# Eight edge columns per comparison in the edge stage of a window-attention and graph-expert kernel

## Chip, cores and metric

One Trainium2 chip, one core. The metric is the device time in microseconds of one execution; of several runs the median is taken.

## What is computed

The input is a (32, 32, 32, 128) tensor: 32 images of 1024 tokens with 128 features. The reference runs two window attentions (the second on shifted windows) and adds them to `x`. Then it runs a graph-attention gate over 32768 nodes and 524288 edges plus 32768 self loops, and four experts mixed by the top two gate scores. The part that matters here is the gate, which reduces over the edges by their destination, and the experts:

```python
src = jnp.concatenate([edge_index[0], loops]); dst = jnp.concatenate([edge_index[1], loops])
e = jax.nn.leaky_relu(a_src[src] + a_dst[dst], negative_slope=0.2)
ee = jnp.exp(e - segment_max(e, dst)[dst]); denom = segment_sum(ee, dst)
agg = segment_sum(h[src] * (ee / denom[dst]), dst) + b_gat
...
hh = jax.nn.gelu(x @ W1[ei] + b1[ei], approximate=False)
out = out + g[..., None] * (hh @ W2[ei] + b2[ei])
```

## The kernel before

Three stages run one after the other: `attention` (windows, node rows, and a sort of the edges by destination), `edges`, and `combine` (gates, mixing, output). The change is in `edges`.

`edges` has 64 passes (`CHUNKS`). The first two and the last two are written out straight, the 60 between them are a hardware loop (`Fori`) of two passes per turn. Each engine has its own order within pass c:

- VectorE (DVE, lines 1336 to 1431 and the pass at the end of that block): `decode(c+1)` turns sorted keys into row numbers `src`; `counts(c)`; `outputs(c)`; `math(c)` with the scans over 68 sorted edges per partition.
- `counts` builds a histogram of the unsorted destinations. A destination is split into its low 7 bits and its high 8 bits. For each of the `HC` = 64 edge columns of a pass, L1418 compares the row 0..127 with the low part, one number per partition, and so writes a one-hot column `ohl` (128x128); L1419 does it for the high part, `ohh` (128x256). Both lie in a ring of `RING` = 8 columns. TensorE multiplies `ohl` by `ohh` (L1651) and accumulates in `cbank`; at the pass's end L1421 adds `cbank` to `hist`.
- TensorE (PE): the 64 one-hot matmuls, then 8 matmuls `hbank` of the experts' first layer (L1658), then 32 matmuls `ybank` of the second (L1667). In fp32 each of these is two loads and two matmuls in the trace. ScalarE (ACT) applies gelu to each `hbank` (L1627, two banks in turn); VectorE adds the bias to each of four `ybank` results (L1431, `yo`).
- GpSimd (POOL): after `decode(c+1)` it issues 68 indirect DMAs (L1602), the gathers of node rows `G` for pass c+1, double-buffered. `math(c)` waits for the gathers of its own pass and for `outputs(c)`, which stands ahead of it on VectorE.
- SyncE (SP) loads keys, destinations and tokens and stores results.

The semaphore `s_oh` tells TensorE of each finished column, `s_ohp` tells VectorE of each multiplied one; a column may be overwritten when the one eight columns back has been multiplied.

Of the kernel before, what the change touches and what calls it, by code (L numbers as in the profile page):

```python
# [21 lines left out]
ALU = mybir.AluOpType  # L22
# [3 lines left out]
P = 128  # L26
# [1133 lines left out]
HC = EDGES // P // CHUNKS  # L1160
# [5 lines left out]
LOW = -1.0e38  # L1166
HI = NODES // P
MCH, LCH, ACH = 0, GHEADS, 2 * GHEADS
RING = 8
CONSTANTS = 9  # L1170
EH = GDIM // GHEADS
VCH = NROW - LCH
# [2 lines left out]
def edges(nc, sorted_keys, node_rows, edge_index, tnT, W1, b1, W2, b2, state_rows, expert_out, endi):  # L1175
# [3 lines left out]
    with ExitStack() as ctx:  # L1179
        def sb(name, shape, dt=F32):  # L1180
            return ctx.enter_context(nc.sbuf_tensor("edge_" + name, shape, dt))
# [4 lines left out]
        def sem(name):  # L1186
            return ctx.enter_context(nc.semaphore("edge_" + name))
# [26 lines left out]
        dlf = sb("dlf", [P, 2, HC])  # L1214
        io = sb("io", [P, HI], I32)
        iob = sb("iob", [P, HI], BF16)
        ohl = sb("ohl", [P, RING, P], BF16)
        ohh = sb("ohh", [P, RING, HI], BF16)
        hist = sb("hist", [P, HI])
# [48 lines left out]
        s_oh = sem("s_oh")  # L1268
        s_ohp = sem("s_ohp")
# [31 lines left out]
        def first_of(b, i, n=1):  # L1301
            return isinstance(i, int) and 2 * i + b < n
# [7 lines left out]
        def _(dve):  # L1310
# [8 lines left out]
            def link(ins, at):  # L1319

                ins.then_inc(s_step, 1)
                st.k += 1
                dve.wait_ge(s_step, at + st.k)
# [83 lines left out]
            def counts(b, i, at):  # L1407
                c = 2 * i + b
                dve.wait_ge(s_dx[b], 16 * i + 16)
                dve.tensor_scalar(dlo[:, 0, :], dx[b][:, :], P - 1, None, ALU.bitwise_and)  # L1410
                link(dve.tensor_scalar(dlo[:, 1, :], dx[b][:, :], 7, None, ALU.logical_shift_right), at)
                link(dve.tensor_copy(dlf[:, :, :], dlo[:, :, :]), at)
                dve.sem_inc(s_dxr, 1)
                for t in range(HC):
                    if t >= RING or not first_of(b, i):

                        dve.wait_ge(s_ohp, c * HC + t - RING + 1)
                    dve.tensor_scalar(ohl[:, t % RING, :], iob[:, 0:P], dlf[:, 0, t:t + 1], None, ALU.is_equal)  # L1418
                    dve.tensor_scalar(ohh[:, t % RING, :], iob[:, :], dlf[:, 1, t:t + 1], None, ALU.is_equal).then_inc(s_oh, 1)  # L1419
                dve.wait_ge(s_ohp, (c + 1) * HC)  # L1420
                dve.tensor_tensor(hist[:, :], cbank[b][:, 0:HI], hist[:, :], ALU.add).then_inc(s_hs, 1)  # L1421

# [216 lines left out]
        @block.tensor  # L1639
        def _(pe):  # L1640
            pe.wait_ge(s_w, 64)

            def body(b, i):
                c = 2 * i + b

                if not first_of(b, i, 2):
                    pe.wait_ge(s_hs, c - 1)
                for t in range(HC):

                    pe.wait_ge(s_oh, c * HC + t + 1)  # L1650
                    pe.matmul(cbank[b][:, 0:HI], ohl[:, t % RING, :], ohh[:, t % RING, :],  # L1651
                              start=(t == 0), stop=(t == HC - 1)).then_inc(s_ohp, 1)

                pe.wait_ge(s_xt[b], 16 * i + 16)
                for k in range(EXPERTS * HB):
                    if k >= 2 or not first_of(b, i):
                        pe.wait_ge(s_ge, c * EXPERTS * HB + k - 1)
                    pe.matmul(hbank[k % 2][:, :], w1[:, k // HB, (k % HB) * P:(k % HB + 1) * P], xt[b][:, :],  # L1658
                              start=True, stop=True).then_inc(s_l1, 1)

                pe.wait_ge(s_ge, (c + 1) * EXPERTS * HB)
                for t in range(UTILES):
                    if t >= 2 or not first_of(b, i):
                        pe.wait_ge(s_y, c * UTILES + t - 1)
                    for x in range(EXPERTS):
                        for h in range(HB):
                            last = pe.matmul(ybank[t % 2][:, x * P:(x + 1) * P], hid[:, x * HB + h, t * P:(t + 1) * P],  # L1667
                                             w2[:, x, h, :], start=(h == 0), stop=(h == HB - 1))
                    last.then_inc(s_l2, 1)

            chunks(pe, body)

            pe.wait_ge(s_hs, CHUNKS)
            pe.wait_ge(s_c, CONSTANTS)
            pe.matmul(hbank[0][:, 0:HI], tri[:, :], hist[:, :], start=True, stop=True)
            pe.matmul(hbank[1][:, 0:HI], ones[:, :], hist[:, :], start=True, stop=True).then_inc(s_pe, 1)
            pe.wait_ge(s_end, mark["x3"])
            for k in range(3):
                last = pe.transpose(cbank[0][0:VCH, k * P:(k + 1) * P], x3[:, k, :], ident[:, :])
            last.then_inc(s_pe, 1)  # L1680
            pe.wait_ge(s_end, mark["V"])
            pe.transpose(cbank[1][:, 0:VCH], most[:, 0:P], ident[0:VCH, 0:VCH])
            pe.transpose(cbank[1][:, VCH:2 * VCH], total[:, 0:P], ident[0:VCH, 0:VCH]).then_inc(s_pe, 1)
# [248 lines left out]
```

## Time and profile before

| | us |
|---|---|
| median of 3 runs | 11302.15 |
| lowest, highest | 11301.26, 11305.25 |
| the profiled execution | 11406.52 |
| its span | 11404.8 |

Engines' busy shares of the span: PE 37%, DVE 47%, ACT 19%, POOL 43%. In the 40 slices of the page, the first seven are the attention stage, the last three or so hold `combine`; the nearly even stretch between is the edge stage. There PE, DVE and POOL are each busy two to four tenths of the time and the granted TensorE clock is half in most slices. So no engine is full there, and a reader must look at one pass in order of time: what each engine does, and what its idle time before each instruction was ended by.

### The profile page before, as it was taken

Reading aid. Unit: us, or ns where it says so; the run is one execution under the profiler, and the core shown is the slowest. Engines: PE = TensorE matmul, PEld = TensorE weight load, DVE = VectorE, ACT = ScalarE, POOL = GpSimd, SP = SyncE. Lnnn points to the kernel's source line nnn. Section 1 sums busy time; section 2 is a strip of 40 time slices with the busy share of each in tenths; the row PEclk is TensorE's granted clock in tenths of the full one; section 3 lists DMA queues with packets and bytes.
Section 4 is the critical chain, followed back from the end, with each engine's and each line's share of the span. In section 5 each row is a group of like instructions: output and inputs, shape, how many; then the busy total and the mean of one; then the engine's idle time right before and its main releaser. Section 6 shows DMA issues by size and latency. Waiting matters only on the chain. (4 is left out here: it accounts for less than half of the span.)

```text
span 11404.8 us, 104675 instructions
## 1 busy us (share of the span) xinstructions
PE 4230.9 (37%) x31385; PEld 2300.7 (20%) x31448; DVE 5397.3 (47%) x14623; ACT 2169.7 (19%) x4631; POOL 4862.3 (43%) x5600
## 2 busy tenths in 40 slices
PE   6899987223222222222222223322222222222300
PEld 4666665011111111111111111111111111111100
DVE  9999998233333333333333333333333333333437
ACT  5777775000000000000000000000000000000015
POOL 3222221644444444444444444444444444444261
PEclk8999998555555555555555555555555555555555
DMA  1222222000001110100000000000110100010147
GB/s 51 59 59 59 59 59 64 16 22 22 22 22 25 27 22 22 22 22 22 22 22 22 22 22 22 22 22 22 29 23 22 22 22 22 22 22 22 32 136 220
DMA packets 503856, 419.15 MB, mean 37 GB/s; under 512 B 160546, under 2 KB 400338, under 8 KB 502866
## 3 DMA queue, kind: packets, MB, share of 16 engines
q1 hardware_dynamic: 355842, 356.89, 9.9%
q0 software_dynamic: 147552, 56.96, 4.3%
q8 instruction: 186, 3.05, 0.1%
q14 instruction: 276, 2.26, 0.1%
HBM read 203.44 MB, written 176.45 MB: 33 GB/s over the span
## 5 line engine op out<-in xcount | busy, mean ns | idle before, releaser
L1602 POOL DMA_INDIRECT edge_G<-node_rows,edge_src x4352 | 4113.1, 945 | 4601.1 <-DVEq L1359 3293.7
L1651 PE MATMUL edge_cbank<-edge_ohh,edge_ohl 128*128 128x256 bf16 x4096 | 1481.1, 396 | 6159.5 <-DVE edge_ohh L1419 5207.8
L1419 DVE TENSOR_SCALAR edge_ohh<-edge_iob,edge_dlf 128x256 bf16<-128x256 bf16 x4096 | 1220.1, 300 | 2169.1 <-issue 2168.9
L1418 DVE TENSOR_SCALAR edge_ohl<-edge_iob,edge_dlf 128x128 bf16<-128x128 bf16 x4096 | 1107.5, 271 | 2159.5 <-issue 2114.5
L1651 PEld LDWEIGHTS edge_cbank<-edge_ohh,edge_ohl 128*128 128x128 bf16 x4096 | 434.4, 106 | 7199.7 <-DVE edge_ohh L1419 5948.5
L1627 ACT ACTIVATE edge_hid<-edge_hbank,edge_b1c 128x512 f32<-128x512 f32 x512 | 351.7, 687 | 7228.5 <-PE edge_hbank L1658 7199.7
L1431 DVE TENSOR_TENSOR edge_yo<-edge_ybank,edge_b2r 128x512 f32<-128x512 f32 x256 | 177.0, 692 | 1003.5 <-PE edge_ybank L1667 940.1
L569 POOL TENSOR_TENSOR attn_nw<-attn_st 128x8 f32<-128x8 f32 x64 | 42.4, 662 | 1409.6 <-DVE attn_st L1024 1409.6
L1658 PE MATMUL edge_hbank<-edge_xt,edge_w 128*128 128x512 f32 x1024 | 601.4, 738 | 29.2 <-ACT edge_hid L1627 16.3
L1667 PE MATMUL edge_ybank<-edge_w,edge_hid 128*128 128x128 f32 x4096 | 477.7, 278 | 76.3 <-ACT edge_hid L1627 62.0
L1667 PEld LDWEIGHTS edge_ybank<-edge_w,edge_hid 128*128 128x128 f32 x4096 | 465.7, 193 | 130.0 <-issue 100.6
L1035 DVE TENSOR_TENSOR attn_keys<-attn_keys 128x1024 f32<-128x1024 f32 (+1 forms) x340 | 477.2, 1404 | 8.7 <-DVE attn_keys L1040 0.5
L1040 DVE TENSOR_TENSOR attn_keys<-attn_keys 128x1024 f32<-128x1024 f32 (+1 forms) x340 | 475.9, 1400 | 0.1
L1125 DVE TENSOR_REDUCE attn_mx<-attn_score 128x16 f32<-128x1024 f32 (+1 forms) x272 | 314.5, 1156 | 86.3 <-PE attn_score L892 52.8
L892 PE MATMUL attn_score<-attn_km,attn_qT 64*64 64x256 f32 x4096 | 293.5, 400 | 86.5 <-DVE attn_S L1127 77.4
L1127 DVE TENSOR_TENSOR attn_S<-attn_score,attn_mx 128x1024 f32<-128x1024 f32 (+1 forms) x272 | 316.0, 1162 | 9.3
L1793 POOL DMA_INDIRECT comb_srow<-state_rows,end_index x256 | 248.1, 969 | 130.8 <-issue 77.4
L926 PE MATMUL attn_out<-attn_vx,attn_pT 128*64 128x34 f32 x8192 | 297.5, 228 | 14.0 <-DVE attn_att L1114 14.0
L911 PE MATMUL attn_turn<-attn_ident,attn_S 128*128 128x128 f32 x2048 | 292.4, 286 | 0.8 <-ACT attn_pT L758 0.8
L758 ACT ACTIVATE attn_pT<-attn_turn 128x1024 f32<-128x1024 f32 (+1 forms) x272 | 268.0, 985 | 130.1 <-PE attn_turn L911 128.0
L751 ACT ACTIVATE attn_S<-attn_S 128x1024 f32<-128x1024 f32 (+1 forms) x272 | 276.9, 1018 | 29.1 <-DVE attn_S L1127 27.4
L1658 PEld LDWEIGHTS edge_hbank<-edge_xt,edge_w 128*128 128x128 f32 x1024 | 205.6, 232 | 378.0 <-ACT edge_hid L1627 272.3
(268 smaller groups left out, 6001.4 us busy)
## 6 DMA issues: line engine op xcount, KB each, us to landing
edge_G<-node_rows,edge_src POOLq DMA_INDIRECT x4352
expert_out<-edge_yo SPq DMA_DIRECT2D x64, 1024.0 KB
comb_ye<-expert_out SPq DMA_DIRECT2D x32, 2048.0 KB
state_rows<-edge_O SPq DMA_DIRECT2D x64, 816.0 KB, 3.6
attn_km<-attn_kT SPq DMA_DIRECT2D x1024, 32.0 KB, 2.0
attn_xin<-in_x SPq DMA_DIRECT2D x32, 512.0 KB, 4.4
attn_xres<-in_x SPq DMA_DIRECT2D x32, 512.0 KB, 5.4
x_rows<-attn_x SPq DMA_DIRECT2D x32, 512.0 KB, 3.4
```

The lines of the kernel that those rows point to most:

```text
L926: last = pe.matmul(out_bank[e * WTOK:(e + 1) * WTOK, j % OUT_SLOTS, c:c + VW], pT[j % 2][:, st, g, e * WTOK:(e + 1) * WTOK], vx[st][:, 2 * ...
L1035: return dve.tensor_tensor(out, a, b, ALU.min)
L1040: return dve.tensor_tensor(out, a, b, ALU.max)
L1125: dve.tensor_reduce(top, scores, AX_X, ALU.max).then_inc(s_mx, 1)
L1127: dve.tensor_tensor(S[j % RING_S][:, :, lo:hi, :, :].rearrange("p a s h k -> p a (s h) k"), scores, top.unsqueeze(3).to_broadcast([P, 2, ( ...
L1418: dve.tensor_scalar(ohl[:, t % RING, :], iob[:, 0:P], dlf[:, 0, t:t + 1], None, ALU.is_equal)
L1419: dve.tensor_scalar(ohh[:, t % RING, :], iob[:, :], dlf[:, 1, t:t + 1], None, ALU.is_equal).then_inc(s_oh, 1)
L1602: pool.indirect_dma_start(G[b][:, t, :], None, node_rows, bass.IndirectOffsetOnAxis(ap=src[b][:, t:t + 1], axis=0)).then_inc(s_g[b][2 * t ...
L1627: act.activation(hid[:, k, :], hbank[k % 2][:, :], ACT.Gelu, bias=b1c[:, k:k + 1]).then_inc(s_ge, 1)
L1651: pe.matmul(cbank[b][:, 0:HI], ohl[:, t % RING, :], ohh[:, t % RING, :], start=(t == 0), stop=(t == HC - 1)).then_inc(s_ohp, 1)
L1658: pe.matmul(hbank[k % 2][:, :], w1[:, k // HB, (k % HB) * P:(k % HB + 1) * P], xt[b][:, :], start=True, stop=True).then_inc(s_l1, 1)
L1667: last = pe.matmul(ybank[t % 2][:, x * P:(x + 1) * P], hid[:, x * HB + h, t * P:(t + 1) * P], w2[:, x, h, :], start=(h == 0), stop=(h == H ...
```

## The change

VectorE no longer compares one column at a time with a number per partition. One `tensor_tensor` compares two broadcast tensors and writes eight columns of `ohl` (128x1024), a second one writes eight of `ohh` (128x2048). The ring grows from 8 to 16 columns. `s_oh` now counts groups of eight, and TensorE waits once per group; it still reports each matmul on `s_ohp`, and VectorE waits before a group until the group two back has been multiplied.

```diff
-RING = 8
+WIDE = 8
+RING = 2 * WIDE
...
-                for t in range(HC):
+                for t in range(0, HC, WIDE):
                     if t >= RING or not first_of(b, i):
 
-                        dve.wait_ge(s_ohp, c * HC + t - RING + 1)
-                    dve.tensor_scalar(ohl[:, t % RING, :], iob[:, 0:P], dlf[:, 0, t:t + 1], None, ALU.is_equal)
-                    dve.tensor_scalar(ohh[:, t % RING, :], iob[:, :], dlf[:, 1, t:t + 1], None, ALU.is_equal).then_inc(s_oh, 1)
+                        dve.wait_ge(s_ohp, c * HC + t + WIDE - RING)
+                    r = t % RING
+                    dve.tensor_tensor(ohl[:, r:r + WIDE, :], iob[:, 0:P].unsqueeze(1).to_broadcast([P, WIDE, P]),
+                                      dlf[:, 0, t:t + WIDE].unsqueeze(2).to_broadcast([P, WIDE, P]), ALU.is_equal)
+                    dve.tensor_tensor(ohh[:, r:r + WIDE, :], iob[:, :].unsqueeze(1).to_broadcast([P, WIDE, HI]),
+                                      dlf[:, 1, t:t + WIDE].unsqueeze(2).to_broadcast([P, WIDE, HI]), ALU.is_equal).then_inc(s_oh, 1)
                 dve.wait_ge(s_ohp, (c + 1) * HC)
...
                 for t in range(HC):
 
-                    pe.wait_ge(s_oh, c * HC + t + 1)
+                    if t % WIDE == 0:
+                        pe.wait_ge(s_oh, c * (HC // WIDE) + t // WIDE + 1)
                     pe.matmul(cbank[b][:, 0:HI], ohl[:, t % RING, :], ohh[:, t % RING, :],
                               start=(t == 0), stop=(t == HC - 1)).then_inc(s_ohp, 1)
```

How the order of the instructions changes on two engines. First VectorE inside the loop, in `counts`, before the change; a REGISTER_ALU works out the number that the wait of L1417 compares with:

```order
L1418 TENSOR_SCALAR edge_ohl<-edge_iob,edge_dlf 128x128
L1419 TENSOR_SCALAR edge_ohh<-edge_iob,edge_dlf 128x256
L1417 REGISTER_ALU
L1418 TENSOR_SCALAR edge_ohl<-edge_iob,edge_dlf 128x128
L1419 TENSOR_SCALAR edge_ohh<-edge_iob,edge_dlf 128x256
```

In the changed kernel VectorE has in `counts`, here in a pass written out straight, from the preparation of the destinations on (of the eight pairs of comparisons the first two are shown):

```order
L1411 TENSOR_SCALAR edge_dlo<-edge_dx 128x64
L1412 TENSOR_SCALAR edge_dlo<-edge_dx 128x64
L1413 CAST edge_dlf<-edge_dlo 128x128
L1420 TENSOR_TENSOR edge_ohl<-edge_iob,edge_dlf 128x1024
L1422 TENSOR_TENSOR edge_ohh<-edge_iob,edge_dlf 128x2048
L1420 TENSOR_TENSOR edge_ohl<-edge_iob,edge_dlf 128x1024
L1422 TENSOR_TENSOR edge_ohh<-edge_iob,edge_dlf 128x2048
```

So 128 comparisons of a pass become 16. TensorE in the loop had, before:

```order
L1650 ISA
L1651 MATMUL edge_cbank<-edge_ohh,edge_ohl 128x256
L1650 REGISTER_ALU
L1651 MATMUL edge_cbank<-edge_ohh,edge_ohl 128x256
L1650 REGISTER_ALU
```

and has now:

```order
L1655 ISA
L1656 MATMUL edge_cbank<-edge_ohh,edge_ohl 128x256 x8
L1655 REGISTER_ALU
L1656 MATMUL edge_cbank<-edge_ohh,edge_ohl 128x256 x8
L1655 REGISTER_ALU
```

The 64 matmuls of a pass stay, each still with its own weight load; seven in eight of the waits, and of the register instructions ahead of them, are gone. No other engine's instructions change.

## Rows read from the trace of the kernel before

**Rows 1.** The page: the span, and busy time of each engine.
```profile
span 11404.8 us, 104675 instructions
PE 4230.9 (37%) x31385; PEld 2300.7 (20%) x31448; DVE 5397.3 (47%) x14623; ACT 2169.7 (19%) x4631; POOL 4862.3 (43%) x5600
```

**Rows 2.** Timeline of POOL: start, duration, idle before and releaser; four gathers.
```profile
2332.27 0.94 POOL L1602 DMA_INDIRECT edge_G<-node_rows,edge_src  x1 [48.14 <-DVEq L1359]
...
5087.93 0.94 POOL L1602 DMA_INDIRECT edge_G<-node_rows,edge_src  x1 [53.35 <-DVEq L1359]
...
5171.69 0.95 POOL L1602 DMA_INDIRECT edge_G<-node_rows,edge_src  x1 [0.30 <-issue]
...
10612.19 0.94 POOL L1602 DMA_INDIRECT edge_G<-node_rows,edge_src  x1 [52.66 <-DVEq L1359]
```

**Rows 3.** Timeline of DVE, the pass that begins at 5087.93.
```profile
5088.26 0.28 DVE L1419 TENSOR_SCALAR edge_ohh<-edge_iob,edge_dlf 128x256 bf16<-128x256 bf16 x1
...
5114.80 0.38 DVE L1418 TENSOR_SCALAR edge_ohl<-edge_iob,edge_dlf 128x128 bf16<-128x128 bf16 x1 [1.11 <-issue]
5116.20 0.29 DVE L1419 TENSOR_SCALAR edge_ohh<-edge_iob,edge_dlf 128x256 bf16<-128x256 bf16 x1 [1.02 <-issue]
...
5183.63 0.28 DVE L1419 TENSOR_SCALAR edge_ohh<-edge_iob,edge_dlf 128x256 bf16<-128x256 bf16 x1
...
5187.22 0.28 DVE L1419 TENSOR_SCALAR edge_ohh<-edge_iob,edge_dlf 128x256 bf16<-128x256 bf16 x1
...
5205.90 0.69 DVE L1431 TENSOR_TENSOR edge_yo<-edge_ybank,edge_b2r 128x512 f32<-128x512 f32 x1 [1.09 <-PE edge_ybank L1667]
```

**Rows 4.** Timeline of ACT: first gelu of that pass; last of the pass begun at 7990.30.
```profile
5189.86 0.69 ACT L1627 ACTIVATE edge_hid<-edge_hbank,edge_b1c 128x512 f32<-128x512 f32 x1 [114.87 <-PE edge_hbank L1658]
5197.65 0.69 ACT L1627 ACTIVATE edge_hid<-edge_hbank,edge_b1c 128x512 f32<-128x512 f32 x1 [0.17 <-PE edge_hbank L1658]
...
8097.55 0.69 ACT L1627 ACTIVATE edge_hid<-edge_hbank,edge_b1c 128x512 f32<-128x512 f32 x1 [0.17 <-PE edge_hbank L1658]
```

**Rows 5.** Timelines of DVE, PE and ACT in the first pass, while 136 gathers run.
```profile
2091.07 0.42 DVE L1419 TENSOR_SCALAR edge_ohh<-edge_iob,edge_dlf 128x256 bf16<-128x256 bf16 x1 [1.16 <-issue]
2109.99 0.42 DVE L1421 TENSOR_TENSOR edge_hist<-edge_cbank,edge_hist 128x256 f32<-128x256 f32 x1 [18.50 <-remote]
...
2098.11 0.40 PE L1651 MATMUL edge_cbank<-edge_ohh,edge_ohl 128*128 128x256 bf16 x1 [2.40 <-remote]
2100.91 0.40 PE L1651 MATMUL edge_cbank<-edge_ohh,edge_ohl 128*128 128x256 bf16 x1 [2.40 <-remote]
...
2132.43 2.07 PE L1658 MATMUL edge_hbank<-edge_xt,edge_w 128*128 128x512 f32 x2 [3.53 <-ACT edge_hid L1627]
...
2131.70 0.69 ACT L1627 ACTIVATE edge_hid<-edge_hbank,edge_b1c 128x512 f32<-128x512 f32 x1 [4.92 <-remote]
2137.29 0.69 ACT L1627 ACTIVATE edge_hid<-edge_hbank,edge_b1c 128x512 f32<-128x512 f32 x1 [4.90 <-remote]
```

**Rows 6.** Windows, first gather to first gap: length, PE, PEld, DVE, ACT, POOL, clock, DMA.
```profile
2199.42:2210.15 10.73, 8.62 (x25) 2.60 (x25) 10.37 (x57) 0.00 (x0) 8.29 (x9) 0.50 0.47 135
5087.93:5096.50 8.57, 5.63 (x16) 1.66 (x16) 7.52 (x40) 0.00 (x0) 6.66 (x7) 0.50 0.20 47
10612.19:10624.26 12.07, 8.82 (x26) 2.62 (x26) 11.07 (x60) 0.00 (x0) 9.33 (x10) 0.50 0.39 115
10824.60:10926.34 101.74, 0.00 (x0) 0.00 (x0) 18.98 (x30) 0.00 (x0) 77.36 (x81) 0.50 0.55 165
```

**Rows 7.** Windows at the end of the pass begun at 5087.93, same columns.
```profile
5187.00:5191.00 4.00, 4.00 (x7) 1.67 (x7) 0.92 (x4) 0.69 (x1) 0.00 (x0) 0.50 0.00 0
5191.00:5193.00 2.00, 2.00 (x4) 0.80 (x3) 0.00 (x0) 0.70 (x2) 0.00 (x0) 0.62 0.00 0
5193.00:5206.60 13.60, 12.02 (x74) 8.41 (x72) 2.77 (x6) 5.39 (x7) 0.00 (x0) 1.00 0.00 0
```

**Rows 8.** Groups by form: `combine` during gathers (10905 to 10926); edge stage (5000 to 6000).
```profile
L1821 DVE TENSOR_TENSOR comb_agg<-comb_srow,comb_l 128x1024 f32<-128x1024 f32 x1 | 1.2, 1226 | 0.0
...
L1397 DVE TENSOR_TENSOR edge_msg<-edge_G,edge_wbank 128x1088 f32<-128x1088 f32 x7 | 19.6, 2794 | 0.0
```

## The prediction
> **What bounds the kernel now.** I read the page first. No engine is full over the span [rows 1], so the order in time decides. POOL's timeline gives the passes: the sixty passes of the loop lie between the first gathers at 2332.27 and 10612.19 [rows 2], so one takes 8279.92 / 60 = 138.0 us. In one pass POOL issues its 68 gathers from 5087.93 to 5171.69 [rows 2], 1.25 us apart, and then waits more than 50 us for VectorE's next decode.
>
> From here on times are offsets from a pass's first gather. VectorE's timeline [rows 3] falls into three. Until about +8.6 the comparisons come as one pair per 0.36 us. Then each one takes 1.40 us from start to start (5114.80, 5116.20) though it is busy for 0.3 to 0.4, and the idle time before it is ended by nothing that the trace names ("issue"). At 5183.63, which is +95.7, the pace is back: ten more pairs to 5187.22 are 0.36 us apart. I call +8.6 to +95.5 the slow stretch. It ends 11 us after the last gather was issued, and 95.5 / 68 is 1.40 us per gather. I read that as something that each gather occupies for 1.40 us, and that lets one instruction of each engine through in that time. After the slow stretch: the remaining columns, eight gelus from +101.9 to +110.4 [rows 4], the last `yo` done at +118.7 [rows 3], the scans, the next decode. Only this tail can shrink, as long as the slow stretch itself keeps its length.
>
> **Who sets the pace in the slow stretch.** This decides the case, and rows 5 show it in the first pass. VectorE starts its last comparison at 2091.07 and is done. TensorE's matmuls still come 2.80 us apart (2098.11, 2100.91), and VectorE learns of the last one only at 2109.99, 9 us later. After that each gelu comes 5.6 us after the one before (2131.70, 2137.29); one gelu needs two loads and two matmuls. So TensorE reports one instruction per 1.40 us, loads and matmuls alike: 2.80 us per one-hot column, 5.6 per gelu. VectorE, with two comparisons per column, has the same 2.80. **The change takes away VectorE's share and leaves TensorE's 64 loads and 64 matmuls.** In the slow stretch a column still costs 2.80 us.
>
> **What precedes the slow stretch.** Rows 6 give the instructions started between the first gather and the first gap. In passes written out straight: 25 + 25 + 57 + 9 = 116 in 10.7 us and 26 + 26 + 60 + 10 = 122 in 12.1 us. In a loop pass 16 + 16 + 40 + 7 = 79 in 8.6 us, to which one register instruction per wait comes, some 38, so 117. In `combine` the first gap stands 101.7 us after the first gather, with 81 + 30 = 111. The count agrees, the time doesn't, so I take the fast beginning to last for about 118 instructions.
>
> **The change part by part.** (1) Comparisons. Each now makes 1024 or 2048 elements. A comparison of two tensors isn't in the edge stage's rows at this size; the nearest are a broadcast multiplication of 1024 elements at 1.23 us, and one of 1088 over strided data at 2.79 us [rows 8]. Operands and results here are dense or broadcast, so I take 1.2 and 2.3, 3.5 us per group of eight, 28 us per pass; the strided row gives 7.9 and 63 us. At the low end the rate of the present comparisons (0.36 us per column) gives 2.9 and 23 us. All three are below 95.5 us, so in the loop the choice costs nothing; the cover is the gathers. Only the last pass has no gathers: there 64 × 0.36 = 23 becomes 28, which **adds 5 us** (up to 40).
>
> (2) Instructions before the slow stretch. A group now has 2 comparisons, 16 loads and matmuls and 2 register instructions, 20 instead of 48. With some 12 others (what SyncE issues, VectorE's rows ahead of the comparisons) and POOL's 0.8 per us, 118 are reached after 4.6 groups, 37 columns, at about +18 instead of 16 columns at +8.6. The other 27 cost 27 × 2.80 = 76 us and are reported by +94.
>
> (3) The end of the slow stretch. Today some ten columns are left at +95.5 and the first gelu comes at +101.9. Now TensorE has multiplied all 64, and the first two `hbank` as well, when it ends: the first gelu starts at +95.7. That is 6.2 us earlier, but not all is kept. The granted clock is 0.50 during the gathers and rises only near +104.6, after some 9 us of unbroken matmuls [rows 7], and a `hbank` takes 2.07 us at the low clock [rows 5]. Four more take until +104.7 and two until +106.6, so the last gelu ends at +107.3 instead of +110.4: **3.1 us saved per pass.** In the pass at 7990.30, whose last gelu ends at +107.9 [rows 4], the same sum with its earlier rise of the clock gives 3.2.
>
> (4) The rest. The ring of 16: VectorE needs the group two back; the report of column 48, the last it waits for, comes at +49, long before it matters. `ybank`, `yo`, the scans and the decode stay as they are. The first pass keeps its time, since its outputs wait for 136 gathers either way. The straight passes at 2199.42 and 10612.19 have only one column left at +95.5 today, and lose about 1.3 us each to the low clock.
>
> **Sum:** 60 × 3.1 = 186, less 2.6 and 5, is 178 us. From the profiled execution's 11406.5 that makes 11228.5; its like runs had a median of 11302.15, 0.9% lower, so the slow stretch must be in them too, and I forecast 11302 − 178 = **11124, say 11125.**
>
> **The rivals.** *A. The gathers hold a port that the new form doesn't need.* The present comparisons are of the one-source kind; rows 3 show them stretched beside gathers, which this would explain. The Trainium skill (SBUF — State Buffer, Who interferes with whom) says that `tensor_scalar` in a 2-port mode and a GpSimd instruction block each other, and that `tensor_tensor` has no such mode, though with two SBUF inputs it still contends with a GpSimd instruction that reads SBUF. By that rule the port is what costs 1.40 us, and VectorE would be free of it. As a mechanism: counts 28 us, gelus and `yo` 17, scans 16, decode 6, together 67, below POOL's 68 × 1.25 = 85 or 95. A pass would take 85 to 95 us and the kernel 8120 to 8720. Against it: during the first 8.6 us the same comparisons run at 0.36 a pair beside gathers [rows 3, 6], and TensorE, which has no part in such a lock, shows 2.80 alone [rows 5]. The same rule's clause on two inputs would let the new comparisons wait for gathers; rows 8 show 1.23 us beside gathers, hence no cost.
>
> *B. Only instructions that report count.* Then a column costs TensorE 1.40 us or less, the one-hots end early, and the gelus run inside the slow stretch at 5.6 us. At +95.5 only `ybank` and `yo` are left, about 10 us with the low clock: last `yo` at +105.6 instead of +118.7, 60 × 13 = 780, so 10520. Rows 5 speak against it: a gelu with one report takes as long as two columns with two. A milder form, more than 45 columns before the slow stretch, saves one or two gelus' time more, to about 10900.
>
> *C. Slower.* The slow stretch begins by time, not by count. Place: column 48. VectorE writes its last group only when column 48 is reported. With 16 columns back at +8.6 that is 8.6 + 32 × 2.80 = +98.2, so the end at +95.5 releases it. Then 3.5 us for the group, which nothing covers, 2.3 for its matmuls and 2.07 for the first `hbank` bring the first gelu to +103.5, and the last ends near +113.1: 2.7 us more per pass, 11475. It decides from 19 columns down (92 us is where the wait must be over). For it: the slow stretch begins between +8.6 and +12.1 in every pass of the edge stage; against it, `combine`'s 101.7 us.
>
> *D. No change.* Savings below 0.4 us a pass: the early gelus lose all they gain to the low clock, for instance if TensorE's pauses between them keep it low for some microseconds longer. That the change does less than it says I leave out: the order shows 16 comparisons for 128.
>
> **How the numbers follow.** Forecast (10,980 to 11,250) 0.50; B and its mild form 0.13; A 0.07; C 0.19; D 0.11. The range reaches from 10850, the mild form of B, to 11450, nearly all of C; beyond lie A, B proper and C's last part, under 0.2 together. Faster by over 0.2% (23 us, about what a measurement of this kernel can tell) has 0.70, within it 0.11, slower 0.19.
>
> **What would show it.** In the changed profile: L1420 near 1.2 and L1422 near 2.3 us, 512 of each; first gathers 134.9 us apart instead of 138.0; a first gelu at +95.7 and a last one ending near +107; PE's one-hot matmuls done well before +95 and the rise of the clock near +104. If first gathers are 95 us apart or less, A holds; with a last `yo` near +105, B; with a group of comparisons after +95.5, C. I am wrong at the root if VectorE's own 112 vanished comparisons shorten the slow stretch itself.

## The result and the profile after

| | before | after |
|---|---|---|
| median, us | 11301.7 (4 runs, 11286.9 to 11305.3) | 10907.96 (4 runs, 10903.5 to 10911.2) |
| profiled execution, us | 11406.5 | 10905.7 |
| mean pass of the loop, us | 138.0 | 129.9 |
| instruction packets (queue q14) | 276 | 95 |

The ratio is 0.9652, interval 0.9637 to 0.9667: 394 us faster where 178 were forecast. The kernel before is slower on the chips that the experiments ran on (11398 to 11409), the changed one hardly (10935.9), and there the ratio is 0.9595 (0.9579 to 0.9611). The two profiled executions differ by 500.8 us, and the account below is of these two; the profiled one of the kernel before is as long as the runs on the experiments' chips and 105 us longer than the runs of the table. The mean pass is worked out from the first gathers of the loop's first pass and of the pass behind the loop: before, 8279.9 / 60; after, (10122.0 − 2325.5) / 60.

The page of the changed kernel, the lines that answer to [rows 1], the instruction queue and two groups (busy time, mean ns, then idle time before):

```profile
span 10903.9 us, 90850 instructions
PE 3927.3 (36%) x31448; PEld 2592.5 (24%) x31448; DVE 5142.4 (47%) x7455; ACT 2174.8 (20%) x4631; POOL 5887.7 (54%) x5600
...
q14 instruction: 95, 0.78, 0.0%
...
L1606 POOL DMA_INDIRECT edge_G<-node_rows,edge_src x4352 | 5132.4, 1179 | 3102.1 <-DVEq L1360 1794.1
```

POOL is busier by 1025 us with the same 5600 instructions; of the others only the loads of TensorE (PEld) grew by much, by 292 us. A gather's mean went from 945 to 1179 ns, although nothing of POOL's was changed. Its timeline in the pass that begins at 4665.46 (start, duration, then idle before and its releaser) says where:

```profile
4665.46 0.95 POOL L1606 DMA_INDIRECT edge_G<-node_rows,edge_src  x1 [29.49 <-DVEq L1360]
...
4670.18 3.03 POOL L1606 DMA_INDIRECT edge_G<-node_rows,edge_src  x1 [0.31 <-issue]
4673.51 3.04 POOL L1606 DMA_INDIRECT edge_G<-node_rows,edge_src  x1 [0.30 <-issue]
...
4693.54 0.95 POOL L1606 DMA_INDIRECT edge_G<-node_rows,edge_src  x1 [0.30 <-issue]
4694.79 0.94 POOL L1606 DMA_INDIRECT edge_G<-node_rows,edge_src  x1 [0.30 <-issue]
```

The first two gathers still take 0.95 us and the third 1.90, then each takes 3.03 us. So ten are issued in the first 28 us where there were 22; from 4693.54 on they are 1.25 us apart again. VectorE's timeline of the same pass, against [rows 3]:

```profile
4673.44 2.29 DVE L1422 TENSOR_TENSOR edge_ohh<-edge_iob,edge_dlf 128x2048 bf16<-128x2048 bf16 x1
4675.64 1.22 DVE L1420 TENSOR_TENSOR edge_ohl<-edge_iob,edge_dlf 128x1024 bf16<-128x1024 bf16 x1
...
4690.12 2.29 DVE L1422 TENSOR_TENSOR edge_ohh<-edge_iob,edge_dlf 128x2048 bf16<-128x2048 bf16 x1
4694.40 0.42 DVE L1425 TENSOR_TENSOR edge_hist<-edge_cbank,edge_hist 128x256 f32<-128x256 f32 x1 [1.98 <-PE edge_cbank L1656]
4708.97 0.69 DVE L1435 TENSOR_TENSOR edge_yo<-edge_ybank,edge_b2r 128x512 f32<-128x512 f32 x1 [14.15 <-remote]
4742.57 0.69 DVE L1435 TENSOR_TENSOR edge_yo<-edge_ybank,edge_b2r 128x512 f32<-128x512 f32 x1 [32.91 <-remote]
4774.77 1.29 DVE L1435 TENSOR_TENSOR edge_yo<-edge_ybank,edge_b2r 128x512 f32<-128x512 f32 x2 [31.51 <-remote]
```

The gathers are slow until the comparisons end, and during these 28 us there is no slow stretch: all 64 columns are multiplied, and `hist` comes at +28.9. The eight gelus follow at once:

```profile
4695.95 0.69 ACT L1631 ACTIVATE edge_hid<-edge_hbank,edge_b1c 128x512 f32<-128x512 f32 x1 [40.86 <-PE edge_hbank L1663]
...
4702.52 0.69 ACT L1631 ACTIVATE edge_hid<-edge_hbank,edge_b1c 128x512 f32<-128x512 f32 x1 [0.17 <-issue]
```

They run from +30.5 to +37.8, mostly at full clock, where the forecast had +95.7. Only then does the slow stretch come, and all that it now hits is `ybank` and `yo`. TensorE's rows show it from the other side:

```profile
4703.33 3.83 PE L1672 MATMUL edge_ybank<-edge_w,edge_hid 128*128 128x128 f32 x32 [0.85 <-issue]
4709.71 3.46 PE L1672 MATMUL edge_ybank<-edge_w,edge_hid 128*128 128x128 f32 x16 [2.54 <-issue]
4743.32 3.71 PE L1672 MATMUL edge_ybank<-edge_w,edge_hid 128*128 128x128 f32 x16 [30.14 <-issue]
```

The multiplication of the second tile ends with the first row, at 4707.16, and VectorE adds its bias at 4742.57; that of the third ends at 4713.17, and VectorE adds its bias at 4774.77, 61.6 us later. **The work isn't slow; the report of it is.** The last two `yo` come at +109.3: ten gathers have started when the eleventh does, at +28.08, and the 58 that are left end, at 1.40 us each, at 28.08 + 81.2 = +109.3. The same sum over all 60 passes of the loop gives +109.9 in the mean, and the last `yo` starts at +110.5 in the mean.

### The profile page after: what moved, and what is told of

Its sections match the earlier page's. It is cut to its first block and busy times, and to the rows that moved or that the text cites. A ratio compares the mean times of both kernels' runs of the same rounds, so it can differ in the third digit from the quotient of the medians.

```text
span 10903.9 us, 90850 instructions
## 1 busy us (share of the span) xinstructions
PE 3927.3 (36%) x31448; PEld 2592.5 (24%) x31448; DVE 5142.4 (47%) x7455; ACT 2174.8 (20%) x4631; POOL 5887.7 (54%) x5600
## 5 line engine op out<-in xcount | busy, mean ns | idle before, releaser
L1606 POOL DMA_INDIRECT edge_G<-node_rows,edge_src x4352 | 5132.4, 1179 | 3102.1 <-DVEq L1360 1794.1
L1656 PE MATMUL edge_cbank<-edge_ohh,edge_ohl 128*128 128x256 bf16 x4096 | 966.5, 417 | 3918.3 <-DVE edge_ohh L1422 3918.3
L1656 PEld LDWEIGHTS edge_cbank<-edge_ohh,edge_ohl 128*128 128x128 bf16 x4096 | 530.1, 141 | 4341.2 <-DVE edge_ohh L1422 4031.8
L1672 PE MATMUL edge_ybank<-edge_w,edge_hid 128*128 128x128 f32 x4096 | 707.7, 348 | 2169.1 <-issue 1847.7
L1672 PEld LDWEIGHTS edge_ybank<-edge_w,edge_hid 128*128 128x128 f32 x4096 | 662.5, 255 | 2250.1 <-issue 1950.5
L1422 DVE TENSOR_TENSOR edge_ohh<-edge_iob,edge_dlf 128x2048 bf16<-128x2048 bf16 x512 | 1169.8, 2285 | 0.0
L1634 ACT ACTIVATE edge_w<-edge_w 128x272 f32<-128x272 f32 x64 | 27.6, 431 | 5005.3 <-DVE edge_w L1392 4867.5
L1420 DVE TENSOR_TENSOR edge_ohl<-edge_iob,edge_dlf 128x1024 bf16<-128x1024 bf16 x512 | 624.7, 1220 | 14.6 <-DVE edge_dlf L1413 14.6
L1663 PE MATMUL edge_hbank<-edge_xt,edge_w 128*128 128x512 f32 x1024 | 568.8, 702 | 0.4 <-ACT edge_hid L1631 0.4
L926 PEld LDWEIGHTS attn_out<-attn_vx,attn_pT 128*64 128x64 f32 x8192 | 269.1, 141 | 63.9 <-issue 43.1
```

What stands on the lines that cost most here:

```text
L926: last = pe.matmul(out_bank[e * WTOK:(e + 1) * WTOK, j % OUT_SLOTS, c:c + VW], pT[j % 2][:, st, g, e * WTOK:(e + 1) * WTOK], vx[st][:, 2 * ...
L1420: dve.tensor_tensor(ohl[:, r:r + WIDE, :], iob[:, 0:P].unsqueeze(1).to_broadcast([P, WIDE, P]), dlf[:, 0, t:t + WIDE].unsqueeze(2).to_broa ...
L1422: dve.tensor_tensor(ohh[:, r:r + WIDE, :], iob[:, :].unsqueeze(1).to_broadcast([P, WIDE, HI]), dlf[:, 1, t:t + WIDE].unsqueeze(2).to_broad ...
L1606: pool.indirect_dma_start(G[b][:, t, :], None, node_rows, bass.IndirectOffsetOnAxis(ap=src[b][:, t:t + 1], axis=0)).then_inc(s_g[b][2 * t ...
```

## The experiments

Theory T: each gather occupies something for 1.40 us through which the other engines' reports also go. Gathers 1.25 us apart leave 0.15 us each behind; the heap of these is the slow stretch. Comparisons of two tensors in SBUF hold the gathers up, to one per 3.3 us, so no heap grows while they run. Rivals: the number of instructions (N), the ring and the waits (W), or a slow stretch that belongs to the gathers at any distance (G). Ratios are to the kernel before on the same chip.

**1. One-column comparisons, the change's ring and waits (narrow).**

```diff
-                    dve.tensor_tensor(ohl[:, r:r + WIDE, :], ...)
-                    dve.tensor_tensor(ohh[:, r:r + WIDE, :], ...).then_inc(s_oh, 1)
+                    for u in range(WIDE):
+                        dve.tensor_scalar(ohl[:, r + u, :], iob[:, 0:P], dlf[:, 0, t + u:t + u + 1], None, ALU.is_equal)
+                        last = dve.tensor_scalar(ohh[:, r + u, :], iob[:, :], dlf[:, 1, t + u:t + u + 1], None, ALU.is_equal)
+                    last.then_inc(s_oh, 1)
```

> The change's waits and ring of 16 stay; the comparisons are again one column each with a scalar operand. Theory T (the form of the comparison does it: a comparison of two tensors in SBUF slows the gathers to one per 3.3 us for 28 us, and a gather that comes later than every 1.40 us leaves the other engines alone): gathers stand 1.25 us apart again, the slow stretch begins near +9 and ends near +95.5, first gelu near +100, time 11250 to 11330. Rival W (the ring of 16 and the wait for each eight do it): 10900 to 10950 and a first gelu near +30. Rival N (the number of instructions does it): 96 instructions fewer is not given here, so also 11250 to 11330: T and N part in the next two runs.

Measured: 11259.6 us, 0.9882 (0.9866 to 0.9899), within the range of T. Gathers are 1.25 us apart throughout, the first gelu comes at +99.7 in the mean, and a pass takes 135.6 us. So the ring and the waits alone give 2.4 us of a pass, not 8. They are some three tenths of the gain and not its main cause.

**2. One-column comparisons of two tensors (narrow_tt).**

```diff
...
+                    for u in range(WIDE):
+                        dve.tensor_tensor(ohl[:, r + u, :], iob[:, 0:P], dlf[:, 0, t + u:t + u + 1].to_broadcast([P, P]), ALU.is_equal)
+                        last = dve.tensor_tensor(ohh[:, r + u, :], iob[:, :], dlf[:, 1, t + u:t + u + 1].to_broadcast([P, HI]), ALU.is_equal)
...
```

> As the run before it, but each one-column comparison is of two tensors in SBUF. As many instructions as the kernel before. T: the gathers are slowed during the comparisons (2 us or more apart), all 64 columns are compared by +30 to +40, the first gelu comes before +45, time 10850 to 11000. N (the number of instructions fills something up): gathers 1.25 us apart or near, slow stretch from about +9, 11250 to 11350.

Measured: 12010.5 us, 1.0541 (1.0522 to 1.0561), outside both expectations. POOL's timeline:

```profile
3531.66 1.10 POOL L1606 DMA_INDIRECT edge_G<-node_rows,edge_src  x1 [0.30 <-issue]
3533.06 30.34 POOL L1606 DMA_INDIRECT edge_G<-node_rows,edge_src  x1 [0.30 <-issue]
3563.70 0.95 POOL L1606 DMA_INDIRECT edge_G<-node_rows,edge_src  x1 [0.31 <-issue]
```

and VectorE's, from the first comparison to the last and on to the pass's last `yo`:

```profile
3528.04 0.29 DVE L1421 TENSOR_TENSOR edge_ohl<-edge_iob,edge_dlf 128x128 bf16<-128x128 bf16 x1 [0.23 <-DVE edge_dlf L1413]
...
3562.17 0.41 DVE L1422 TENSOR_TENSOR edge_ohh<-edge_iob,edge_dlf 128x256 bf16<-128x256 bf16 x1
...
3652.19 1.29 DVE L1435 TENSOR_TENSOR edge_yo<-edge_ybank,edge_b2r 128x512 f32<-128x512 f32 x2 [26.63 <-remote]
```

The first four gathers, beside the first comparisons, take their usual time or little more; the fifth lasts 30.34 us, until the comparisons end. The mechanism is T's: the gather is held up, and no slow stretch delays the one-hots (the first gelu starts 2.6 us behind the next gather in the mean). The size isn't: T had one gather per 3.3 us. T's own sum then gives the loss: this pass begins at 3527.88, the sixth gather starts at +35.8, and the 63 that are left end, at 1.40 us each, at +124.0; the last two `yo` start at +124.3. Why eight columns per instruction let one gather through per pair and one column per instruction lets none through is open. The waits on `s_ohp` between groups of eight are the same in both kernels, and VectorE shows no idle time at them in either. That the count of instructions matters (N) can't explain a gather of 30 us.

**3. The change with the edge columns in PSUM (psum_wide).**

```diff
-                link(dve.tensor_copy(dlf[:, :, :], dlo[:, :, :]), at)
+                dlp = wbank[:, GHEADS * TC:GHEADS * TC + 2 * HC].rearrange("p (a t) -> p a t", a=2)
+                link(dve.tensor_copy(dlp, dlo[:, :, :]), at)
```

and `dlp` for `dlf` in both comparisons.

> The change as it is, but the tensor of edge columns that is compared lies in PSUM, so one input is in SBUF and one in PSUM. T: the gathers are not slowed by it (1.25 us apart from the first), the slow stretch begins when about 118 instructions have started and ends at +95.5, which is the world that the forecast described: about 11125, 11050 to 11200. N (few instructions are enough, the slowed gathers are a side effect that only costs): as after or better, a first gelu near +30 and gathers 1.25 us apart, 10700 to 10910. If the gathers are slowed here too (3.3 us apart), the place of the second input doesn't matter and the time is that of the change, 10908.

Measured: 11044.4 us, 0.9692 (0.9676 to 0.9708), a pass of 132.0 us; that is 6 us below the range of T. POOL's timeline, and VectorE's below it:

```profile
4707.57 0.94 POOL L1607 DMA_INDIRECT edge_G<-node_rows,edge_src  x1 [0.30 <-issue]
4708.82 0.95 POOL L1607 DMA_INDIRECT edge_G<-node_rows,edge_src  x1 [0.30 <-issue]
```

```profile
4721.01 2.28 DVE L1423 TENSOR_TENSOR edge_ohh<-edge_iob,edge_wbank 128x2048 bf16<-128x2048 bf16 x1
4727.55 1.22 DVE L1421 TENSOR_TENSOR edge_ohl<-edge_iob,edge_wbank 128x1024 bf16<-128x1024 bf16 x1 [4.26 <-remote]
...
4746.51 1.22 DVE L1421 TENSOR_TENSOR edge_ohl<-edge_iob,edge_wbank 128x1024 bf16<-128x1024 bf16 x1 [15.54 <-remote]
...
4768.91 1.22 DVE L1421 TENSOR_TENSOR edge_ohl<-edge_iob,edge_wbank 128x1024 bf16<-128x1024 bf16 x1 [18.98 <-remote]
...
4801.85 0.42 DVE L1426 TENSOR_TENSOR edge_hist<-edge_cbank,edge_hist 128x256 f32<-128x256 f32 x1 [29.52 <-remote]
```

The comparisons take as long as in the changed kernel (2.28 and 1.22), but the gathers stay 1.25 us apart. This is in the main the world of the forecast: five groups, 40 columns, are compared before the first wait; then a group comes per 19 to 22 us, at 2.4 to 2.8 a column (the last group at +62.6, where the forecast had its release at +49); the stretch ends at +95.5 and the first gelu starts at +95.6. This kernel and the changed one differ by where one operand lies, and by the slowed gathers. Without the slowed gathers the change gives 6.0 us of a pass, of which the ring and the waits are 2.4; the slowed gathers give the other 2.1.

**4. A short clearing behind every gather (fill).**

```diff
+                    pool.memset(junk[:, t, :], 0.0).then_inc(s_junk, 1)
```

with 32 elements, behind each of the 68 gathers; ahead of each pass's first gather POOL also waits until all clearings of the passes before are done.

> The change, and behind every gather POOL clears 32 elements of a buffer that nobody reads (some 0.2 us), so that gathers stand 1.45 us or more apart instead of 1.25. T: with every gather later than 1.40 us behind the one before there is no slow stretch at all; VectorE and TensorE go through counts, outputs and scans in about 70 us beside the gathers, the pass is set by POOL, 28 us of slowed gathers and the rest at 1.45, near 115 us instead of 131.5: 9800 to 10100. Rival G (the slow stretch belongs to the gathers as such, whatever their distance): the stretch gets 0.2 us per gather longer or stays, and the time is 10900 to 11800.

Measured: 10801.7 us, four executions from 10691 to 10890, 0.9479 (0.9402 to 0.9557), outside both expectations. It is no test of pacing: the 0.14 us fitted into the 0.30 that lie between gathers anyway, and their distance stayed 1.258 us in the median. The profiled execution is the one of 10691 us, and POOL's first gathers of three passes show that its loop has two regimes:

```profile
2307.67 0.95 POOL L1610 DMA_INDIRECT edge_G<-node_rows,edge_src  x1 [3.01 <-remote]
...
3384.49 0.95 POOL L1610 DMA_INDIRECT edge_G<-node_rows,edge_src  x1 [8.46 <-DVEq L1362]
...
5077.34 1.99 POOL L1610 DMA_INDIRECT edge_G<-node_rows,edge_src  x1 [22.81 <-DVEq L1362]
```

The first ten passes, from 2307.67 to 3384.49, take 107.7 us each: POOL goes on almost without a break. The fifty behind them take 130.3 us, as in the changed kernel, and in them POOL waits more than 20 us for the next decode. The gain of this execution over the changed kernel lies in those ten passes, which would also make a wide spread if their number differs between executions; only this one's trace is on record. What tips the loop from one regime to the other is open. Late in such a long pass POOL's rows are these:

```profile
5019.24 0.95 POOL L1610 DMA_INDIRECT edge_G<-node_rows,edge_src  x1 [0.75 <-issue]
...
5022.03 0.95 POOL L1610 DMA_INDIRECT edge_G<-node_rows,edge_src  x1 [1.49 <-issue]
```

In the slow stretch POOL is now held up itself, and gathers come 1.3 to 2.8 us apart for a while. In the long passes that gains nothing.

**5. The changed kernel again (after_again),** for the chip's level.

> The changed kernel unchanged, so that it stands beside the others of this chip: 0.957 to 0.966 of the kernel before; the kernel before has been 11302 on one chip and 11398 on another, and this says whether the change's own time moves with it.

Measured: 10935.9 us, 0.9595 (0.9579 to 0.9611), a pass of 130.2 us.

**6. Pacing by 256 elements (pace256).**

```diff
+                    if t > 0 or not first_of(b, i):
+                        pool.wait_ge(s_junk, c * TC + t)
+                    pool.sem_inc(s_pace, 1)
+                    pool.memset(junk[:, :], 0.0).then_inc(s_junk, 1)
```

The buffer and the two semaphores are declared above. POOL waits for its own last clearing and clears again; no other engine waits for either semaphore.

> The change, and behind every gather POOL clears 256 elements (0.31 us in the page of the kernel before) and steps a semaphore, so that gathers outside the comparisons stand 1.42 to 1.5 us apart. In the run with 32 elements the clearing of 0.14 us fitted in the gap, the distance stayed 1.258, and nothing of the theory was tested. T (a gather every 1.40 us or later leaves the other engines alone): 28 us of slowed gathers and 58 at 1.45, a pass of some 113 to 118 us instead of 130, no pause over 5 us between yo instructions, 9900 to 10250. G (the slow stretch belongs to the gathers whatever their distance): yo instructions 30 us apart as before, pass 130 us or more, 10900 to 11500.

Measured: 9958.4 us, 0.874 (0.8726 to 0.8755), a pass of 115.0 us. Gathers stand 1.445 us apart behind the comparisons, and VectorE's `yo` rows are these:

```profile
4341.97 0.69 DVE L1438 TENSOR_TENSOR edge_yo<-edge_ybank,edge_b2r 128x512 f32<-128x512 f32 x1 [11.73 <-PE edge_ybank L1679]
4344.60 0.69 DVE L1438 TENSOR_TENSOR edge_yo<-edge_ybank,edge_b2r 128x512 f32<-128x512 f32 x1 [1.93 <-PE edge_ybank L1679]
4348.29 0.69 DVE L1438 TENSOR_TENSOR edge_yo<-edge_ybank,edge_b2r 128x512 f32<-128x512 f32 x1 [3.00 <-PE edge_ybank L1679]
4353.39 0.69 DVE L1438 TENSOR_TENSOR edge_yo<-edge_ybank,edge_b2r 128x512 f32<-128x512 f32 x1 [4.41 <-remote]
```

Four starts within 11.4 us; in the changed kernel it takes 65.8 us to the third alone. Slower gathers, 0.2 us each, and the kernel is 9% faster than the changed one. G is out.

**7 and 8. Both, with 256 and with 512 elements (psum_pace256, psum_pace512).**

> Both: edge columns in PSUM, so that the comparisons don't slow the gathers, and gathers paced by clearing 256 elements. T: 68 gathers at 1.45 is 99 us, all else beside them, a pass of 100 to 106 us: 9050 to 9500. G: 11000 to 11700.

Measured: 9027.5 us, 0.7924 (0.7911 to 0.7937), a little below the range of T, a pass of 100.1 us. The first gelu starts at +49.6 and the last `yo` ends at +79.1 in the mean, both well inside the gathers.

> As the last, with 512 elements, gathers 1.6 to 1.7 us apart. T: 68 x 1.65 is 112 us, so slower than with 256 elements by some 10 us a pass: 9800 to 10100. If 1.45 us is too near to 1.40 for the other engines' own instructions to get through, this one is the faster of the two. G: 11100 to 12200.

Measured: 9894.8 us, 0.8684 (0.867 to 0.8699), a pass of 113.95 us: 68 × 1.658 is 112.7. POOL now sets the pass alone, and of the two distances 1.66 us is too long: the other engines don't need it.

**9. The kernel before, with nothing but the pacing (before_pace256).**

> The kernel before, with its one-column comparisons and ring of 8, and nothing but the pacing of the gathers (clearing 256 elements, 1.44 us apart). T: the slow stretch is gone here too, though VectorE and TensorE issue as many instructions as before; comparisons 0.36 us a pair, 64 in 23 us, all beside the gathers, a pass of 68 x 1.44 = 98 to 100 us, 8980 to 9080, the same as with the wide comparisons in PSUM: the change would then be worth nothing. N (the number of instructions matters even so): 128 comparisons and 64 waits more keep part of the slow stretch, 9300 to 11000.

Measured: 9069.6 us, 0.7956 (0.7942 to 0.7969), a pass of 100.95 us. The groups of VectorE and POOL:

```profile
L1605 POOL DMA_INDIRECT edge_G<-node_rows,edge_src x4352 | 4198.8, 965 | 791.4 <-POOL edge_junk L1611 510.4 <-issue 280.9
L1611 POOL MEMSET edge_junk<- 128x256 f32 x4352 | 1475.9, 339 | 2.3
```

```profile
L1421 DVE TENSOR_SCALAR edge_ohl<-edge_iob,edge_dlf 128x128 bf16<-128x128 bf16 x4096 | 1365.7, 338 | 155.2 <-issue 109.5 <-DVE edge_dlf L1415 17.2 <-PE edge_cbank L1658 12.7
```

The same line in the kernel before:

```profile
L1418 DVE TENSOR_SCALAR edge_ohl<-edge_iob,edge_dlf 128x128 bf16<-128x128 bf16 x4096 | 1107.5, 271 | 2159.5 <-issue 2114.5
```

The idle time before this line's instructions was 2159.5 us and is 155.2 here, with the same 4096 instructions. That rules out N as the cause: the instructions are all there, the slow stretch isn't. The clearing is 0.34 us and its result is never read. The first gelu comes at +45 to +66 (+57.5 in the mean), later than the 23 us of comparisons that were expected, so some reports still come late; it costs little, for POOL sets the pass.

**10. Below 1.40 (before_pace128).** The same with 128 elements.

> The same with 128 elements, gathers some 1.34 us apart, below 1.40. T, with a fixed 1.40 us per gather: what is left over grows by 0.06 us a gather instead of 0.15, so the slow stretch starts later and is shorter, some 20 to 50 us of a pass, or POOL is held back itself now and then; 8900 to 9800, between before_pace256 and before, and certainly slower gathers than asked for. If the pass is 68 x 1.34 = 91 us, 8500, there is no threshold near 1.40 and the theory has the wrong number.

Measured: 10539.2 us, 0.9239 (0.9224 to 0.9254), a pass of 124.4 us. Asked for 1.34 us, gathers start so and then are held up:

```profile
4433.02 0.95 POOL L1605 DMA_INDIRECT edge_G<-node_rows,edge_src  x1 [0.16 <-issue]
4434.36 0.95 POOL L1605 DMA_INDIRECT edge_G<-node_rows,edge_src  x1 [0.17 <-issue]
...
4454.29 0.97 POOL L1605 DMA_INDIRECT edge_G<-node_rows,edge_src  x1 [0.46 <-issue]
4456.40 0.95 POOL L1605 DMA_INDIRECT edge_G<-node_rows,edge_src  x1 [0.39 <-issue]
```

The mean distance within a pass is 1.407 us, and the first `yo` starts at +95.8 in the mean, so the slow stretch ends where it ended before. The two runs differ by nothing but the length of the clearing. The time went above the 9800 that I had as the upper bound, so I had the cost of falling short of 1.40 too low: 0.1 us per gather between this run and the last is worth 1470 us.

**11. `combine` paced too (both).** The lines of run 6 behind each gather of `combine`.

> before_pace256, and the 256 gathers of the last stage (combine) are paced in the same way. Their slow stretches (VectorE's instructions 1.40 us apart there) go: 20 to 80 us less than before_pace256. If VectorE in combine waits for the gathers' data or for the 2 MB loads, nothing or 20 us more.

Measured: 8983.3 us, 0.7877 (0.7864 to 0.789), 86 us less than run 9 on the same chip, a little more than the 80 that were expected at most. The waits of VectorE for `comb_res`, which the trace puts down to "remote", were 112.6 us in run 9 and are gone from the list; the one for the first gathers' data grew:

```profile
DVE comb_l L1832 <- DMA comb_srow<-state_rows,end_index: 161.4, 4, 104.2
```

**12. All together (psum_both):** wide comparisons from PSUM and both stages paced.

> Wide comparisons with the edge columns in PSUM, the edge stage's gathers and combine's gathers paced with 256 elements each: the sum of what psum_pace256 has over before_pace256 (some 0.3 to 0.4%) and of what combine's pacing brings (86 us): 8930 to 8960.

Measured: 8936.6 us (8930 to 8942), 0.7838 (0.7825 to 0.7852). This is the fastest version: 22% below the kernel before, and 0.7838 / 0.9595 = 0.817 of the changed one.

## Why the prediction was right and wrong

**The step that failed** is the price of the comparisons in step 1, "in the loop the choice costs nothing; the cover is the gathers", and with it the premise that "the slow stretch itself keeps its length". The runs showed in its place that the comparisons hold the gathers up (3.03 us for 0.95). So all one-hots and gelus are through by +37.8 at normal pace, the slow stretch comes later, is shorter and ends at +109.3 instead of +95.5, and the last `yo` ends at +111.2 instead of +117.9. And where the gathers aren't slowed (run 3), the change gives 6.0 us of a pass and not the 3.1 of the forecast: step 3 was 1.6 us short and step 4 left out 1.3.

**The slow stretch's cause** held as far as the runs reach. "Something that each gather occupies for 1.40 us" is borne out from both sides: at 1.44 us between gathers the stretch is gone (9070), at 1.34 it is there (10539), and in the changed kernel it ends 58 × 1.40 us behind the last slowed gather. But I took it for a given and wrote "only this tail can shrink, as long as the slow stretch itself keeps its length". It doesn't keep it.

**Step 1, the comparisons,** had the durations right (1220 and 2285 ns for 1.2 and 2.3) and the price wrong. The cover was not there, for the comparisons stop what was to cover them. [rows 8] say what VectorE's instruction takes beside gathers, and it takes nothing more. POOL's own rows of the same microseconds, in the kernel before, say what the gathers pay:

```profile
10908.32 1.49 POOL L1793 DMA_INDIRECT comb_srow<-state_rows,end_index  x1 [0.30 <-issue]
...
10911.49 0.95 POOL L1793 DMA_INDIRECT comb_srow<-state_rows,end_index  x1 [0.30 <-issue]
10912.75 1.19 POOL L1793 DMA_INDIRECT comb_srow<-state_rows,end_index  x1 [0.30 <-issue]
```

Beside `combine`'s operations on two tensors (10907.77 to 10910.37, with the one of [rows 8], 10911.89 to 10914.37 and 10919.63 to 10923.37) single gathers take 1.49, 1.19 and 1.18, while the others there take 0.94 to 1.07. The loser of the meeting was POOL, by less than the 2 us of the changed kernel. The Trainium skill (SBUF — State Buffer, Who interferes with whom), which the prediction cites under rival A, says that an instruction of VectorE with two SBUF inputs contends with a GpSimd instruction that reads SBUF, and one with at most one SBUF input, outside the modes that take both ports, doesn't. The runs agree with the line it draws: with one input in PSUM 0.94 us a gather, with two in SBUF 3.03, and 30.34 for the one that meets the one-column comparisons. That the first gathers beside the comparisons run at their usual pace isn't explained by it. I had asked of the rule only what VectorE would wait.

**Step 2, 118 instructions and then 2.80 per column,** described the PSUM version well (40 columns compared, for 37) and the first part of the changed kernel's pass not at all: in its first 28 us, without a gap, stand 152 instructions even without register ones. The windows' row (PE, PEld, DVE, ACT, POOL) is

```profile
4665.46:4693.54 28.08, 14.28 (x62) 7.99 (x63) 26.79 (x16) 0.00 (x0) 25.03 (x11) 0.50 0.17 47
```

What fills up seems to do so only while gathers come faster than one per 1.40 us; in the four places of the prediction they stood 1.25 us apart. Counted from +28.08, where they do so here, the number fits again: 108 instructions with the register ones start until TensorE ends the first `ybank` tile, the first whose report is late (done at 4705.38, `yo` at 4708.97). That is one pass; why it is a number of instructions stays open.

**Step 3, first gelu at +95.7 and 3.1 us saved per pass.** In the changed kernel the first gelu is at +30.5 and the last `yo` ends at +111.2 in the mean, where it was +117.9: 6.7 us. In the PSUM version, where the step's premises hold, the first gelu is at +95.6, the last gelu ends at +105.0 (forecast +107.3) and the last `yo` at +113.2, 4.7 us before the old place. So even there the step was 1.6 us short: the clock rises at +100.9 in the mean, not near +104.6. I had carried over "some 9 us of unbroken matmuls" from [rows 7]; the windows of the PSUM version show it sooner (the column behind the busy times is the granted clock):

```profile
4801.85:4806.00 4.15, 3.37 (x5) 1.50 (x6) 0.42 (x1) 1.95 (x3) 0.00 (x0) 0.56 0.00 0
4806.00:4818.00 12.00, 11.15 (x73) 8.18 (x71) 2.08 (x3) 4.72 (x6) 0.00 (x0) 1.00 0.00 0
```

**Step 4, "the rest stays"** missed 1.3 us per pass. From the last `yo` to the next first gather it is 20.1 us in the mean before and in run 1, and 18.8 after and in the PSUM version. The list of VectorE's waits of the kernel before, 2300 to 9000, has the difference:

```profile
DVE edge_dst L1345 <- issue: 80.9, 24, 3.6
```

24 pauses of 3.4 us, one in two passes, before the first row of `decode`. In the changed kernel that row waits 0.45 us in the mean (23.4 us in 52 passes). All six kernels with 128 comparisons a pass have it (before and runs 1, 2, 9, 10 and 11), and none of those with 16. The instruction packets go with it as long as the gathers aren't paced: 276 and 275 where the pause is, 95 and 95 where it isn't (paced kernels, with more rows on POOL, have 277 to 462). The Trainium skill (Runtime: NRT & Kernel Launch, Instruction fetch mechanics) says that a taken branch to a target outside the two pages held forces a fetch before execution goes on; the trace agrees as far as it can, since 112 rows fewer per pass of VectorE ended both, but no run changes the code's length alone.

**The passes outside the loop.** The last pass was to cost 5 us more, and the straight pass ahead of it 1.3; from that pass's first gather to the first gather of `combine` it is 1.2 us more (212.41 to 213.65). Why it isn't 6.3 is open. The straight passes ahead of the loop were to stay or lose 1.3 us, and gained 13. `combine` itself was 12 us shorter in the profiled execution of after and 2 in that of run 5, so that part is chance.

The sum of what was measured: 60 × 8.06 = 483 in the loop (6.76 before the last `yo` and 1.29 behind it), 13 in the straight passes ahead of it and the 12 of `combine`, less 6 by which the edge stage began later and 1 behind the loop, gives 501, as much as the profiled executions differ. The forecast was for the runs of the table, which differ by 394. Against the profile of run 5 the difference is 474, of which 466 are the loop's. No trace shows the kernel before on a chip where it takes 11302, so where the 100 us go is open; 30 pauses of 3.4 us would be as much, but that such a run lacks them isn't shown.

**The rivals.** C (slower, 0.19) and D (0.11) didn't come. A's price was far off, but its sentence on two inputs held the mechanism. B had the picture, the one-hots end early and at +95.5 only `ybank` and `yo` are left, and gave 13 us a pass, with some 10 us left behind the slow stretch. What came was that picture by another cause: the slow stretch ends 13.8 us later, and 1.9 us are left behind it. The forecast's total lay 217 us above the result and inside its range. That it lay inside is luck: the range was made of other mechanisms, and none of them had the slowed gathers.

## What to carry to other kernels

Where one engine's transfers come faster than something behind them can take, find the distance at which nothing is left over, and pace the issuing engine to it: 0.34 us of useless work per gather made this kernel 20% faster, more than any change of the work around it that was tried. When two engines meet at a port, read both engines' rows in the same microseconds, since the one that you change may be the one that doesn't wait. And a gain of this kind should be tried again once the cause is mended: paced, the change with both inputs in SBUF is 9.8% slower than the kernel before paced (0.874 to 0.7956), and with one in PSUM 0.4% faster (0.7924, on another chip; 0.5% with `combine` paced too).

## What the runs showed of the hardware that I had not expected

- Reports, not work, are late. With gathers 1.25 us apart, TensorE's third tile was done 61.6 us before VectorE went on with it. At 1.44 us apart the delay is mostly gone, at 1.34 us it is there.
- POOL can be held up as well: with a clearing of 32 elements between gathers they come up to 2.8 us apart in the slow stretch, without one they stay 1.25 us apart throughout.
- VectorE's comparisons of two SBUF tensors hold gathers up. With one column each (0.28 and 0.41 us) a gather was stopped for 30.34 us; with eight columns each (1.22 and 2.29 us) one gather gets through per pair, 3.33 us. VectorE's durations show nothing of it: with one input in PSUM they are 1.22 and 2.28 us.
- What it is that takes 1.40 us per gather is open. It isn't the data: the DMA engines' mean share is 0.07 to 0.10 in the slow stretch, and in the pass at 5087.93 the last packet of the gathers' queue starts 2 us behind the last gather's start, 10 us before the slow stretch ends. No run has gathers of fewer rows or through another queue. Loads and matmuls that step no semaphore count as well ([rows 5]: a gelu per 5.6 us, for two loads and two matmuls). So it may be that the profiler's own records take part: every execution here has a span and a granted clock from the profiler, and no run shows the slow stretch, or the gain by pacing, without it.
- The kernel before differs by 0.9% between chips, the changed one by 0.25%. No run says why.
